# Attention's preparation, its finish and the edge sort of a graph network on one core: more gathers issued ahead, a product with its operands swapped, loads moved ahead of a stage

## What is computed

```python
x = x + gnn0(layernorm(x))      # agg[src] += weight * (x @ W_l)[dst]; out = agg + b + x @ W_r + b
x = x + moe_top1(layernorm(x))  # 8 experts, capacity, 256 -> 1024 -> 256
x = x + gatv2(layernorm(x))     # attention over the edges, 4 heads of 64
x = x + moe_top2(layernorm(x))  # 8 experts, two of them per token, 256 -> 512 -> 256
```

```python
x_l = x @ W_l + b_l;  x_r = x @ W_r + b_r          # per node, 4 heads
e = x_l[src] + x_r[dst] + ea @ W_e                 # per edge, plus one loop edge per node
logits = einsum(leaky_relu(e, 0.2), att)           # per edge and head
out = softmax over the edges of a node, times x_l[src], summed per node
out = elu(out + x @ W_res + bias)
```

## Time and profile before

| | |
|---|---|
| median of three runs | 2737.9 us (2734.44 to 2755.3) |
| the profiled execution, its own time | 2739.46 us |
| its span, first to last instruction | 2737.4 us |
| prepare / convolve and top-1 experts | 239.7 / 916.3 us |
| attend_prepare / attend / attend_finish | 121.8 / 1049.7 / 94.9 us |
| top-2 experts | 315.0 us |
| busy share of PE, DVE, ACT, POOL over the span | 86%, 68%, 54%, 46% |

### The profile page before, as it was taken

How to read it: one execution, slowest core, us unless ns; L and a number is a source line. 1 busy time by engine, 2 the same in 40 slices (tenths; PEclk the granted TensorE clock), 3 DMA queues, 4 the chain that set the end, 5 groups by cost and what they waited for, 6 DMA issues and landing times. The chain is left out here.

```text
span 2737.4 us, 60486 instructions
## 1 busy us (share of the span) xinstructions
PE 2355.9 (86%) x16667; PEld 1940.7 (71%) x16667; DVE 1850.2 (68%) x6928; ACT 1470.4 (54%) x4615; POOL 1271.6 (46%) x1302
## 2 busy tenths in 40 slices
PE   5985869999885988877999999999999999437994
PEld 3884537876652655534999999999999998316993
DVE  8785799999877235254666666666666666775334
ACT  1782004444431222244888888888888888633441
POOL 1235777777772776033444444444444442004551
PEclk8686589999996999988999999999999999568997
DMA  5303434444433345133322222222222232451224
GB/s 175 100 30 99 104 94 101 102 103 103 106 98 124 104 154 170 56 106 116 79 72 72 72 72 72 72 72 72 72 72 72 72 72 39 145 187 59 70 72 158
DMA packets 252450, 259.39 MB, mean 95 GB/s; under 512 B 143396, under 2 KB 202815, under 8 KB 251876
## 3 DMA queue, kind: packets, MB, share of 16 engines
q0 software_dynamic: 57344, 151.11, 19.9%
q1 hardware_dynamic: 191476, 101.18, 13.2%
q10 hardware_dynamic: 3312, 3.28, 0.3%
HBM read 196.38 MB, written 59.06 MB: 93 GB/s over the span
## 5 line engine op out<-in xcount | busy, mean ns | idle before, releaser
L2293 POOL DMA_INDIRECT l_rows<-xl_tab,l_ra x454 | 441.2, 972 | 574.5 <-DMA l_ra<-rec_a 464.3
L2434 DVE CUSTOM_DVE_ANT_0 l_junk<-l_ps_lb,l_pen 128x256 bf16<-128x256 f32 x908 | 331.4, 421 | 281.8 <-PE l_ps_lb L2396 281.6
L1014 POOL DMA_INDIRECT room_a<-h_tab,c_rec x432 | 439.0, 1016 | 138.2 <-issue 78.0
L1061 PE MATMUL c_ps<-room_a 128*128 128x256 f32 x864 | 309.4, 447 | 84.4 <-DVE room_a L1343 49.5
L1061 PEld LDWEIGHTS c_ps<-room_a 128*128 128x128 f32 x864 | 160.0, 210 | 184.7 <-DVE room_a L1343 131.5
L1031 ACT ACTIVATE s_cum<-iota_f,c_row_f 128x128 f32<-128x128 f32 x391 | 122.7, 389 | 312.0 <-PE c_ps_s L1099 205.8
L2366 PE MATMUL l_ps_ag<-l_val,l_hot 128*128 128x260 f32 x908 | 256.4, 405 | 0.3 <-issue 0.3
L2331 ACT ACTIVATE l_val<-l_rows,l_val 128x64 f32<-128x64 f32 x908 | 241.7, 337 | 7.4
L2321 ACT ACTIVATE room_a<-room_a,l_cexp x908 | 241.3, 345 | 1.1 <-issue 1.1
L2356 PE MATMUL l_bank_l<-g_att_d,l_rz 128*128 128x4 f32 x1816 | 240.5, 253 | 0.3 <-ACT l_rz L2343 0.3
L2396 PE MATMUL l_ps_lb<-ident,l_ls 128*128 128x128 f32 x1816 | 235.2, 273 | 0.0
(11 more groups left out here) (597 smaller groups left out, 5506.6 us busy)
## 6 DMA issues: line engine op xcount, KB each, us to landing
m_w<-in_L_ffn_w SPq DMA_DIRECT2D x16, 1024.0 KB, 7.9
rec_a<-room_a SPq DMA_DIRECT2D x114, 102.0 KB
l_ra<-rec_a SPq DMA_DIRECT2D x227, 51.0 KB, 2.1
e_w<-in_L_ffn_W SPq DMA_DIRECT2D x16, 512.0 KB, 12.5
l_rows<-xl_tab,l_ra POOLq DMA_INDIRECT x454, 3.0
room_a<-h_tab,c_rec POOLq DMA_INDIRECT x432, 2.8
xrr_tab<-q_xrr SPq DMA_DIRECT2D x25, 256.0 KB, 2.0
f_xrr<-xrr_tab SPq DMA_DIRECT2D x5, 1280.0 KB, 13.3
```

Of the source, the lines that this page charges most:

```text
L1014: pool.indirect_dma_start(rows[:, u, :], None, K["h_tab"], bass.IndirectOffsetOnAxis(ap=rec[:, n % RSLOTS, k, 0:1].bitcast(I32), axis=0)). ...
L1061: pe.matmul(ps[s % NB][:, :], hot[:, u, :], rows[:, s % RU, :], start=True, stop=True).then_inc(s_agg, 1)
L2293: pool.indirect_dma_start(rows[:, u, j, :], None, K["xl_tab"], bass.IndirectOffsetOnAxis(ap=ra[:, u, j, A_SRC:A_SRC + 1].bitcast(I32), axi ...
L2434: dve.tensor_tensor_reduce(junk[:, h, :], ps_lb[:, h, :], pen[:, v3, :], 1.0, -3.0e38, ALU.add, ALU.max, tmax[:, v3, h:h + 1]).then_inc(S[ ...
```

## The change

Four edits, in four phases:

- **prepare**: the product of L681 has its operands swapped: `hot_f`'s 64 columns are the weights, `hot_r`'s 128 columns move, and the sum stands transposed, [64, 128], in PSUM. After a chunk ACT copies it to SBUF (`turned_g`), PE transposes it back (`ps_back`), and ACT copies code and weight from there one iteration later (k % 3 == 1 in place of 0). DVE decodes in iteration k % 3 == 2 in place of 1. PE's transposition stands in its queue behind the next chunk's first batch and ahead of the next node tile.
- **attend_prepare**: POOL issues 18 gathers at the start in place of 10, and gather 18 + s in its loop; DVE's order at the start is arrive, variance, ready of group 0, then of group 1, then arrive of group 2.
- **attend**: in step 197 of 227 (`EARLY_AT`), SP issues four more DMAs behind the load of that step's records: `xl` and `xrr` of groups 0 and 1 of attend_finish.
- **attend_finish**: SP loads only groups 2 to 4. PE's `ps_la` has two buffers in place of three; `ps_lin` is split: the first group's 5 tiles (10 passes) after its products, the other 20 tiles (40 passes) after the second group's, each in its own bank, and DVE waits for the one that it needs.

```diff
@@ prepare, ACT @@
                 if k and k % PER == 0:
                     g = k // PER - 1
                     act.wait_ge(s_mm, k)
-                    act.activation(of(code_i, g), ps_g[g % 2][:, 0:SLOTS], ACT.Copy).then_inc(s_code, 1)
+                    wait(act, s_back, g - 1)
+                    act.activation(turned_g[:, g % 2, :], ps_g[g % 2][0:FQ, 0:P], ACT.Copy).then_inc(s_turn, 1)
+                if k % PER == 1 and k > 1 or k == len(BATCHES):
+                    g = (k - 1) // PER - (1 if k < len(BATCHES) else 0)
+                    act.wait_ge(s_back, g + 1)
+                    act.activation(of(code_i, g), ps_back[g % 2][:, 0:SLOTS], ACT.Copy).then_inc(s_code, 1)
                     act.wait_ge(s_blank, 7)
-                    act.activation(recs[:, g, :, 2], ps_g[g % 2][:, SLOTS:2 * SLOTS], ACT.Copy).then_inc(s_wcol, 1)
+                    act.activation(recs[:, g, :, 2], ps_back[g % 2][:, SLOTS:FQ], ACT.Copy).then_inc(s_wcol, 1)
@@ prepare, PE @@
                     for col in range(first, end):
-                        mm = pe.matmul(ps_g[g % 2][:, 0:2 * SLOTS], hot_r[:, k % HR, col - first, :],
+                        mm = pe.matmul(ps_g[g % 2][0:FQ, 0:P],
                                        hot_f[:, k % 2, col - first, :, :].rearrange("p f q -> p (f q)"),
+                                       hot_r[:, k % HR, col - first, :],
                                        start=(col == STARTS[g]), stop=(col == STARTS[g + 1] - 1))
                     mm.then_inc(s_mm, 1)
+                if k % PER == 0 and k:
+                    g = k // PER - 1
+                    pe.wait_ge(s_turn, g + 1)
+                    wait(pe, s_code, g - 1)
+                    wait(pe, s_wcol, g - 1)
+                    pe.transpose(ps_back[g % 2], turned_g[:, g % 2, :], ident[0:FQ, 0:FQ]).then_inc(s_back, 1)
@@ prepare, DVE @@
-                    if g and k % PER == 1:
+                    if g and k % PER == 2:
                         decode(g - 1)
@@ attend_prepare @@
-            FIRST = GROUPS[2][1]
+            FIRST = GROUPS[3][1] + 3
...
             arrive(0)
             variance(0)
+            ready(0)
             arrive(1)
-            ready(0)
             variance(1)
+            ready(1)
             arrive(2)
-            ready(1)
@@ attend, SP @@
+                if s == EARLY_AT:
+                    for k in range(FIN_EARLY):
+                        some = slice(k * FIN_CT, (k + 1) * FIN_CT)
+                        sp.dma_start(A["xl_e"][:, some, :], node_rows(K["xl_tab"], k)).then_inc(K["s_fin"][k], 16)
+                        sp.dma_start(A["xrr_e"][:, some, :], node_rows(K["xrr_tab"], k)).then_inc(K["s_fin"][k], 16)
@@ attend_finish @@
-            for k in range(NC):
+            for k in range(FIN_EARLY, NC):
...
-                if n == NPC - 1:
-                    pe.wait_ge(s_lac, len(GROUPS_T))
-                    for tile in range(NT):
-                        mm = pe.matmul(ps_lin[:, tile, :], lat[:, tile, :], A["wea"][0:ED, :], start=True, stop=True)
+                if n in (NPC - 1, 2 * NPC - 1):
+                    late = n != NPC - 1
+                    for tile in range(CT, NT) if late else range(CT):
+                        pe.wait_ge(s_lac, tile // PER + 1)
+                        mm = pe.matmul(ps_lin[late][:, tile, :], lat[:, tile, :], A["wea"][0:ED, :], start=True, stop=True)
                     mm.then_inc(s_lin, 1)
```

More of the change, by code:

```diff
@@ L397, in prepare @@
         ps_g = [c.enter_context(nc.psum_tensor(f"p_ps_g{k}", [P, 512], F32)) for k in range(2)]
+        FQ = 2 * SLOTS
+        turned_g = t("turned_g", [FQ, 2, P], F32)
+        ps_back = [ps[:, 0:FQ] for ps in ps_s[0:2]]
         ps_col = ps_g[0][:, 0:4 * NT].rearrange("p (k b) -> p k b", b=NT)
@@ L2487, in attend_finish, with rows_of, xl, xrr @@
         x, ident = K["x"], K["ident"]
-        CT = 5
+        CT = FIN_CT
         NC = NT // CT
         AGW = HEADS * (HC + 1)
-        xl = t("xl", [P, NT, ROW_L], F32)
-        xrr = t("xrr", [P, NT, 2 * D], F32)
+        xl_late = t("xl", [P, NT - FIN_EARLY * CT, ROW_L], F32)
+        xrr_late = t("xrr", [P, NT - FIN_EARLY * CT, 2 * D], F32)
+        def rows_of(early, late, first, n):
+            return early[:, first:first + n, :] if first < FIN_EARLY * CT else late[:, first - FIN_EARLY * CT:
+                                                                                    first - FIN_EARLY * CT + n, :]
+        def xl(first, n):
+            return rows_of(A["xl_e"], xl_late, first, n)
+        def xrr(first, n):
+            return rows_of(A["xrr_e"], xrr_late, first, n)
         room = A["xr_p"][:, :, :, :].rearrange("p t k d -> p (t k d)").bitcast(F32)
@@ L2505, in attend_finish @@
         NPC = len(PAIRS) // NC
-        ps_la = [c.enter_context(nc.psum_tensor(f"f_ps_la{k}", [ED, PER, P], F32)) for k in range(3)]
-        ps_lin = c.enter_context(nc.psum_tensor("f_ps_lin", [P, NT, HEADS], F32))
+        ps_la = [c.enter_context(nc.psum_tensor(f"f_ps_la{k}", [ED, PER, P], F32)) for k in range(2)]
+        ps_lin = [c.enter_context(nc.psum_tensor(f"f_ps_lin{k}", [P, NT, HEADS], F32)) for k in range(2)]
         ps_z = [c.enter_context(nc.psum_tensor(f"f_ps_z{k}", [P, 2, D], F32)) for k in range(4)]
@@ L2511, in attend_finish @@
         s_lin, s_co, s_sc = (sem("f_" + n) for n in ("lin", "co", "sc"))
-        s_in = [sem(f"f_in{k}") for k in range(NC)]
+        s_in = K["s_fin"]
         block = c.enter_context(nc.Block(no_gpsimd_drain=True))
@@ L2532, in _ @@
                 act.wait_ge(s_lap, n + 1)
-                act.activation(lat[:, g[0]:g[-1] + 1, :], ps_la[n % 3][:, 0:len(g), :], ACT.Copy).then_inc(s_lac, 1)
+                act.activation(lat[:, g[0]:g[-1] + 1, :], ps_la[n % 2][:, 0:len(g), :], ACT.Copy).then_inc(s_lac, 1)
             for k in range(NC + 2):
@@ L2548, in _ @@
                 if k >= 2:
-                    neg = xl[:, tiles(k - 2), 0:D]
+                    neg = xl((k - 2) * CT, CT)[:, :, 0:D]
                     act.wait_ge(s_n, k - 1)
@@ L2558, in _ @@
             for n, g in enumerate(GROUPS_T):
-                wait(pe, s_lac, n - 2)
+                wait(pe, s_lac, n - 1)
                 for k, tile in enumerate(g):
-                    mm = pe.transpose(ps_la[n % 3][:, k, :], la[:, tile, :], ident[:, :])
+                    mm = pe.transpose(ps_la[n % 2][:, k, :], la[:, tile, :], ident[:, :])
                 mm.then_inc(s_lap, 1)
@@ L2611, in _ @@
                     o.then()
-                    o.did(dve.tensor_tensor(lg[:, ts, :], lg[:, ts, :], xl[:, ts, D:ROW_L], ALU.add))
-                    dve.wait_ge(s_lin, 1)
+                    o.did(dve.tensor_tensor(lg[:, ts, :], lg[:, ts, :], xl(k * CT, CT)[:, :, D:ROW_L], ALU.add))
+                    dve.wait_ge(s_lin, min(k, 1) + 1)
                     o.then()
-                    o.did(dve.tensor_tensor(lg[:, ts, :], lg[:, ts, :], ps_lin[:, ts, :], ALU.add))
+                    o.did(dve.tensor_tensor(lg[:, ts, :], lg[:, ts, :], ps_lin[min(k, 1)][:, ts, :], ALU.add))
                     o.then()
```

30 lines of the change are left out of this document (18 added, 12 removed).

## The result

The changed kernel took 2708.81 us in the median of four runs (2707.28 to 2716.15), the kernel before 2736.65 beside it: a ratio of 0.9905, 95% interval 0.9886 to 0.9924. The forecast was 2702 in a range of 2682 to 2726. The profiled execution took 2709.53 us, 29.9 less than the one of before; the forecast for that pair was 36 less.

| us | prepare | convolve, top-1 | attend_prepare | attend | attend_finish | top-2 |
|---|---|---|---|---|---|---|
| before | 239.73 | 916.51 | 121.61 | 1049.66 | 94.91 | 314.98 |
| after | 227.39 | 916.65 | 103.10 | 1052.41 | 92.09 | 315.86 |
| difference | -12.3 | +0.1 | -18.5 | +2.8 | -2.8 | +0.9 |
| forecast | -12 | 0 | -19 | 0 | -5 | 0 |

What follows compares the result with a forecast made beforehand. It took the phases to stand in a row, three of the edited ones filled by no single engine. -12 - 19 - 5 = -36 us on the profiled 2739.5 gives 2703, written 2702 for the median; range 2682 to 2726.

Steps and rivals of the forecast that it cites:

- Part 1: prepare's sort product with swapped operands: -18 us from the clock, +6 for added work, together -12 (-20 to +11).
- I expect 2.4 GHz for most of the loop and take two thirds, -18: Prepare's loop: sets moving twice the columns keep PE's clock up; -18 us, ends 0 and -26.
- I take 5: Prepare, six chunks without `places`: DVE waits for the later code, about 1.8 us each; cost 5 us, between 0 and 11.
- In the chunks with `places` PE idles 2.65 us there anyway, so they are hidden: Prepare's loop: work queued behind PE's new wait for ACT's copy costs nothing in these chunks.
- The clock did not stay as it was: Rival in prepare's sort: PE's clock stays as before, making that phase's change +6 us and the total 2720; chance 0.20.
- The clock falls: Rival in prepare's sort: PE stops for ACT's copy every chunk, all sets run slow, +50 us, total 2764; chance 0.04.
- More is regained: Rival: 2.4 GHz throughout prepare's loop (-24), decoding hidden, no clock fall in attend_prepare (-22); total 2686; chance 0.14.
- Part 2: attend_prepare's earlier gathers: three waits go (-13), clock holds (-4), sooner start (-2); together -19 us (-12 to -23).
- The rival that eighteen gathers slow each other: attend_prepare: gathers arrive no sooner, 9 us of gain lost, total 2711; chance 0.10 shared with the early-loads rival.
- Part 3: attend_finish: `ps_lin` split saves 3.4 us, first load 0.4, short DVE waits go; together -5 us (-1 to -7).
- Part 4: attend's early loads: 3.95 MB take 10.4 us ahead of step 198's records, covered by 22 us of lead; cost 0.
- POOL's wait for records past 5 us: Sign in attend near step 198 that would show the forecast wrong.

## Why the prediction was right, and where not

**Part 1: the sum came out, its terms did not.** "I expect 2.4 GHz for most of the loop and take two thirds, -18" was too little. In the loop of the changed kernel 1.2 GHz is left for about 14 us (0.54 over 9 us, 0.70 over 10) of the 67, so that by the prediction's own conversion (26 us for 67) some 20 us were regained. "I take 5" for the decoding was the term that was mis-sized: it allowed a delay of at most 1.8 us in each of six chunks, 11 in all, and took the waits of before to be gone. DVE waited in nine, 2.7 us on average, 24.0 in all; moving the decoding alone brought 10.6, the upper bound. "In the chunks with `places` PE idles 2.65 us there anyway, so they are hidden" weighed PE alone; once the clock held, PE, DVE and ACT were busy 65.8, 65.7 and 68.1 of the 76 us from 124 on, so there was little left for a wait of DVE's to hide behind. And one term was not there at all: SP's 114 fills stand ahead of the stores that free ACT's buffers, a floor at 109 us that the slower loop hardly touched (ACT waited for a store 0 to 0.9 us there, 3.6 to 6.3 here). The prediction asked which queues a moved step passes, not what a faster loop runs into; it cost 6.6 us (230.2 to 223.61; 6.2 by the medians). The -12 that the pair of profiles shows is also 5 us of luck; the mean over eight profiles is -7.

**The rivals of part 1.** The clock did not stay as it was and did not fall (sets of 2.40 us, 0.94 over the loop). "The clock falls" rests on a miscount: of the sets of before 11, and one in part, ran slow, not "some 16", and its 2764 leaves out the +6 of the same part, so it would have been some 2780; the forecast does not use it. "More is regained" was nearly right on the clock and wrong on "with the decoding hidden": with the decoding moved and the fills spread, prepare is 216.9, 20 us below the mean of before.

**Part 2 held, step by step.** The three waits are gone (13.2 forecast), PE's stall is 2.42 us where 2.1 was named as what stays, the clock no longer falls in the groups: 5.8 us a group, 18.5 in all, 103.1 us where "near 102" stood. At the start the first tile was normalised 8.0 us into the phase in place of 11.0 and the third 12.6 in place of 18.5, but the fourth 19.1 in place of 20.2: 1 us of the 2 forecast. The rival that eighteen gathers slow each other fell.

**Part 3: the mechanism was right, one bound was left out of the sum.** "A wait of 0 to 5 us for the second part may come, by whether its passes run at 0.11 or 0.21": they ran at 0.21 and the wait was 2.94 us. Both ends were there, and the sum took the near one, though of the 50 passes before, which took 7.56 us, part had run at 0.21 already. Of six profiles with this part as it was made, three took 91.9 to 92.1 us and three 94.8 to 95.0; in these the second group's wait was 4.6 us, the passes having been slow from earlier on. Without this part the phase has two lengths too: 94.9 us in four profiles, and 97.3 in the one of decoding later in the kernel before, where the fifty passes took 9.90 us. Like against like the part is worth 2.3 to 2.8 us. With the forty cut, the phase takes 89.3 to 90.3, the 5 us that were forecast.

**Part 4 held, one of its signs did not.** Zero cost, by the lead. The 22 us, though, were read to DVE's use at 2308.7; the first reader of the records is POOL's gather, and the trace of before has its last at 2292.7. The gather issued at 2143.61 was for rows that PE took from 2157.99 on, so 14 us of lead were left behind the wait. "POOL's wait for records past 5 us" was named as a sign of failure and came (11.87), without failure: the wait of an engine ahead of the bound is no loss until it has used up the lead, so the sign to look for was PE's idle time.

**What is left of the 6 us** between forecast (-36) and pair (-29.9): attend's later clock 2.8, attend_finish 2.2, the last phase 0.9. None was in the rivals; the first is an accident of when the clock rises, of either sign.

## What to carry to other kernels

When an edit makes one engine faster in a loop, list what the loop will now reach early: each wait of the engine that comes next, and each queue whose old work the loop used to arrive behind (here SP's fills; of some 20 us that the clock gave, 13 were lost to them and to DVE's wait for the code). Before pricing from one profile, see how far the same phase moves between profiles: 5 us in prepare and nearly 4 in attend, here as much as the terms forecast. And a wait named as a sign of failure should be one of the engine that bounds the stage.

## What the runs showed of the hardware that I had not expected

- The granted clock can fall under a PE that the profile shows without a gap. In attend_finish PE was busy for all of 21.9 us at a clock of 0.53, with passes of 16 rows and 4 or 256 columns, so the prediction's "wherever wide passes follow one another it is at 2.4" is too wide. In the sort, passes of 64 moved columns fell to 1.2 GHz every second chunk where as many passes of 128 columns, beside waits no shorter, did so less or not (0.93 to 1.00 from 124 to 200 us in place of 0.87).

```profile
2309.90:2331.80 21.90, 21.90 (x76) 18.55 (x75) 15.92 (x35) 9.29 (x39) 0.00 (x0) 0.53 0.38 137
```

- The clock rises at moments that the instructions alone do not set: with the same ones in attend's first 17 us it rose at 10.4 to 11.0 us or at 16.1 to 17.0 us, 3 us of time apart. The changed kernel itself did both: 16.4 us in its first profile, 10.5 in its second, where the clock rose in the first of these two stretches (attend began at 1252.42). Thirteen idle passes on PE at the stage's start brought it to 3.6 to 6.0.

```profile
1262.42:1263.42 1.00, 0.74 (x6) 0.52 (x4) 0.00 (x0) 0.57 (x2) 0.69 (x2) 0.74 0.23 83
1263.42:1264.42 1.00, 0.92 (x9) 0.92 (x10) 0.00 (x0) 0.93 (x4) 0.69 (x2) 1.00 0.50 133
```

- DVE's addition of 1280 elements from two tensors in SBUF took 2.02 us in place of 1.49 where POOL's addition of 0.78 us had started 0.1 us ahead of it. Without the gathers' wait it now starts just behind POOL's in each of groups 3 to 5. An addition of 5 elements took 0.69 just behind POOL's, in the kernel before too (the last line), and 0.15 where POOL had no addition running (1163.02):

```profile
1176.31 0.78 POOL L2105 TENSOR_TENSOR q_xrr<-q_xrr,q_xlo 128x256 f32<-128x256 f32 x1 [1.56 <-DVE q_rest L2217]
...
1181.74 0.77 POOL L2105 TENSOR_TENSOR q_xrr<-q_xrr,q_xlo 128x256 f32<-128x256 f32 x1 [2.47 <-DVE q_rest L2217]
1181.84 0.69 DVE L260 TENSOR_TENSOR mean_a<-stats_a 128x5 f32<-128x5 f32 x1
...
1163.02 0.15 DVE L260 TENSOR_TENSOR mean_a<-stats_a 128x5 f32<-128x5 f32 x1
...
1198.30 0.69 DVE L258 TENSOR_TENSOR mean_a<-stats_a 128x5 f32<-128x5 f32 x1
```

The Trainium skill has the rule for it (SBUF — State Buffer, Who interferes with whom: a DVE instruction with two inputs in SBUF contends with a GpSimd instruction that reads SBUF, and the later one blocks); the rows agree, with half a microsecond each time.
